# The next batch's context attention, stepped through the present batch's tail in a fused decoder layer

## The reference

```python
def layer(x, ctx):                                   # per batch
    # 1. self attention, 16 heads of 16, with clipped relative positions (+-20)
    h = layernorm(x)
    attn = softmax((q @ k.T + q . rel_k[idx]) / 4)
    x = x + (attn @ v + attn . rel_v[idx]) @ Wo.T + bo
    # 2. context attention WITHOUT softmax: 16 heads of 64
    Qn = layernorm(layernorm(x)) * g1 + b1
    Kn = layernorm(ctx) * g1 + b1                    # 1601 rows
    qn, kn = l2norm(Qn @ wq), l2norm(Kn @ wk)        # by head
    out = (qn @ kn.T) @ (Kn @ wv)                    # = qn @ (kn.T @ Kn @ wv)
    y = Q + out @ wo + bo
    x = x + y + gelu(layernorm(y) * g2 + b2 @ w1 + b1) @ w2 + b2
    # 3. gated FFN, inputs and weights rounded blockwise (16) to FP4 values
    z = quant(layernorm(x))
    x = x + quant(silu(z @ wg.T) * (z @ wu.T)) @ wd.T
```

## Time and profile before

| | us |
|---|---|
| median of 3 runs | 3678.69 |
| lowest, highest | 3668.11, 3689.46 |
| profiled execution | 3670.19 |
| its span, first to last instruction | 3668.3 |
| period of the loop over the batches | 440.3 |

### The profile page before, as it was taken

The page is one execution under the profiler, slowest core; times in us unless marked ns, Lnnn a source line. Parts: engine busy times, 40 slices in busy tenths (PEclk is TensorE's granted clock), DMA queues, the critical chain, the costliest instruction groups (busy, mean ns, idle before and its releaser), DMA issues.

```text
span 3668.3 us, 48646 instructions
## 1 busy us (share of the span) xinstructions
PE 2691.3 (73%) x14836; PEld 1813.0 (49%) x14884; DVE 1985.8 (54%) x4001; ACT 1195.6 (33%) x1925; POOL 1153.9 (31%) x812
## 2 busy tenths in 40 slices
PE   0487777877787776867768777687777867787776
PEld 0255544554455544555445545355544554455544
DVE  5646465463754537545375554646455464654537
ACT  1226222271233612344123432225223271233611
POOL 1352223422243123521235222362223522244122
PEclk9999988998899987998879989799888998899987
DMA  6365004650056400663008520364104650056400
GB/s 195 34 127 135 20 6 53 123 145 7 2 85 124 112 6 13 100 128 82 6 18 127 120 58 6 32 137 126 28 6 48 128 141 6 8 76 127 118 6 6
DMA packets 503886, 259.07 MB, mean 71 GB/s; under 512 B 213166, under 2 KB 501702, under 8 KB 502598
## 3 DMA queue, kind: packets, MB, share of 16 engines
q1 hardware_dynamic: 436982, 221.53, 31.0%
q10 hardware_dynamic: 66560, 33.56, 4.0%
HBM read 129.67 MB, written 125.35 MB: 70 GB/s over the span
## 4 chain that ended last, share of the span: by engine, by line
PE 50%; DVE 19%; issue 10%; ACT 8%; POOL 4%; DMA 4%; ACTq 1%; DVEq 1%; POOLq 0%; another core or an unknown queue 0%
PE PS L1273 44%; PE PS L1276 7%; DMA bias_scr<-M 4%; DVE arena L422 3%; ACT arena L862 2%; ACT arena L869 2%; DVE arena L427 2%; DVE arena L419 2%; POOL rn L367 1%; POOL rstd L367 1%; POOL arena L439 1%; DVE PS L1115 1%; DVE arena L424 1%; DVE arena L1072 1%; DVE arena L429 1%
## 5 line engine op out<-in xcount | busy, mean ns | idle before, releaser
L1276 PE MATMUL PS<-ident,arena 128*128 128x128 f32 (+1 forms) x3356 | 571.3, 299 | 628.5 <-POOL arena L439 289.8
L1276 PEld LDWEIGHTS PS<-ident,arena 128*128 128x128 f32 (+1 forms) x3356 | 410.9, 152 | 822.4 <-POOL arena L439 313.0
L1273 PE MATMUL PS<-arena 128*17 128x128 f32 (+5 forms) x6624 | 729.5, 318 | 106.6 <-ACT arena L869 60.1
L1273 PEld LDWEIGHTS PS<-arena 128*17 128x17 f32 (+2 forms) x6656 | 510.2, 126 | 214.1 <-ACT arena L869 68.1
L367 POOL TENSOR_TENSOR rn<-rn,mhalf 128x16 f32<-128x16 f32 (+1 forms) x136 | 412.9, 3036 | 475.0 <-DVE rn L1065 264.7
L1115 DVE CUSTOM_DVE_ANT_0 PS<-PS,arena 128x512 f32<-128x512 f32 x512 | 343.2, 712 | 97.0 <-PE PS L1273 68.9
L1273 PE MATMUL PS<-cwk,arena 128*128 128x512 f32 (+1 forms) x832 | 376.1, 595 | 23.7 <-ACT arena L801 21.0
L862 ACT ACTIVATE arena<-PS,nmax 128x512 f32<-128x512 f32 x512 | 352.1, 690 | 74.3 <-DVE nmax L1115 65.5
L716 POOL TENSOR_TENSOR arena<-arena,mass_mask 128x512 f32<-128x512 f32 x128 | 163.3, 1276 | 571.9 <-ACT arena L862 571.9
L367 POOL TENSOR_TENSOR rstd<-rstd,mhalf 128x1 f32<-128x1 f32 (+3 forms) x153 | 104.0, 680 | 719.6 <-DVE rstd L380 300.9
L1063 DVE TENSOR_REDUCE ss<-arena 128x16 f32<-128x1024 f32 (+1 forms) x104 | 126.9, 1220 | 285.1 <-ACT arena L807 285.1
(11 more groups left out here) (163 smaller groups left out, 3763.2 us busy)
## 6 DMA issues: line engine op xcount, KB each, us to landing
arena<-bias_scr SPq DMA_DIRECT2D x128, 336.0 KB, 3.2
prob_scr<-arena SPq DMA_DIRECT2D x128, 336.0 KB, 3.7
bias_scr<-M ACTq DMA_DIRECT2D x64, 512.0 KB, 4.8
q_scr<-arena SPq DMA_DIRECT2D x128, 128.0 KB
arena<-k_scr SPq DMA_DIRECT2D x64, 256.0 KB, 10.9
arena<-q_scr SPq DMA_DIRECT2D x128, 128.0 KB, 3.2
arena<-in_ctx SPq DMA_DIRECT2D x96, 128.0 KB, 2.5
arena<-far_scr SPq DMA_DIRECT2D x64, 182.0 KB, 17.0
```

The costliest lines, as they stand in the source:

```text
L1273: return pe.matmul(o, l, r, start=start, stop=stop, **kw)
L1276: return pe.transpose(o, i, ident[0:i.shape[0], 0:i.shape[0]])
```

## The change

The context of a batch no longer stands in a stage of its own. While batch b is in its tail, the engines work on the context of batch b+1, and while b is in its FFN, they run the finale and the preparation of b+1. Batch 0 gets its context and preparation ahead of the loop. The loop also does this work for a ninth batch of zeros (`ctx` and `x` are padded), in the last turn.

- The context runs in two passes of half the heads each: 26 steps (`CSTEPS`) with 512 projected columns and 4 matmuls into two banks of `G` (4, 5). Norm and transposition of a row tile are done in the first pass only; all 13 normed tiles stay in SBUF. The second pass waits until the banks have been copied out (`evac_g`).
- One pipeline turn over all engines is a `slot(nb, s)`, s from -6 to 25. `SLOTS_AT` says behind which piece of the tail each engine runs which slots. A slot on PE is the projection of step s+3, the transposition of tile s+4 and the `G` matmuls of step s; on DVE it is statistics of tile s+6, head sums of step s+2, norm of tile s+5, scaling of step s+1.
- The tail uses PSUM banks 0 to 3 (and half of 7) in place of eight: `project_q` has one pair of banks, not two.
- The finale is laid between the four tiles of the second MLP matmul. Then come `norm_x(b+1)`, the projections, the splits (`first_rests`, `second_rests`, `middle_parts`, `last_parts`), strewn between the rounding steps of x. `gate_up` comes behind them.
- SP's list for b+1 is `prepare`: band stores, all part stores, a wait for `parts_stored`, then the loads of `Kp`, `Qp`, `Kfar`, and only then the stores of the far edges, which ACT issued before. There are 16 of them now, of 128 x 512 (`Eb` has half the room).
- POOL makes the 16 far edges in the rounding loop, four behind each tile's `quant_divide` and `quant_finish`.

```diff
+SLOTS_AT = {("band", 0): (-6, -5), ("band", 1): (-4,), ("band", 2): (-3,), ("band", 3): (-2,),
+            ("wo", 0): (-1,), ("wo", 1): (0,), ("wo", 2): (1,), ("wo", 3): (2,), "ln": (3, 4, 5, 6),
...
+            "yn": (19, 20, 21), ("h", 1): (22,), ("h", 3): (23,), ("h", 5): (24,), ("h", 7): (25,)}
...
 # POOL
                 for t in range(T + 1):
                     if t < T:
                         pool.wait_ge(quant_s, 2 * (T * b + t + 1) + 1)
                         pool.sem_inc(waits_alone, 1)
-                        quant_divide(pool, gs[:, t, :], t % 2, 128, FF)
+                        quant_divide(pool, gs[:, t % 2, :], t % 2, 128, FF)
                     if t:
...
+                        quant_finish(pool, st, qc[:, (t - 1) % 2, :], (t - 1) % 2, 128, FF, NQ0 + b * QPB + NXQ + t - 1)
+                    if t < T:
+                        for g in range(NG):
+                            far_edge(b + 1, t, g)
...
+            def far_edge(nb, t, g):
+                if t == 0 and g == 0:
+                    pool.wait_ge(r_act, 2 * T * (nb + 1) + 1)
...
+                    pool.wait_ge(part2_ready, 2 * (nb + 1) + 1)
...
+                pool.wait_ge(eb_stored[g % 2], 16 * (2 * (T * nb + t) + g // 2) + 1)
...
+                pool.tensor_tensor(Eb[:, g % 2, :, :], tail_mask[:].unsqueeze(1).broadcast_to([128, HG, 128]),
+                                   bcast(Rb[:, t, g * HG:(g + 1) * HG, BAND], 128), ALU.mult).then_inc(eb_ready, 1)
 # PE, FFN
+                second(0)
+                transpose_g(b + 1)
+                second(1)
+                key_values(b + 1)
+                second(2)
+                context_out(b + 1)
+                second(3)
+                project_x(b + 1)
...
 # DVE, FFN
+                add_x2(3)
+                norm_x2(0)
+                norm_x(b + 1)
+                quant_count(dve, st, 0, 128, XQ * E, NQ0 + b * QPB)
+                norm_x2(1)
+                first_rests(b + 1)
+                quant_count(dve, st, 1, 128, XQ * E, NQ0 + b * QPB + 1)
+                second_rests(b + 1)
                 for t in range(T + 3):
...
+                    if t == 0:
+                        last_parts(b + 1)
```

More of the change, by code:

```diff
@@ L851, in exps, with slots @@
+            all_slots(slot, 0)
+            evac_g(0, 1)
+            copy_gt(0)
+            copy_m(0)
+            project_x(0)
+            for t in range(T):
+                copy_r(0, t)
+            middle_parts(0)
+            with act.Fori(0, NB) as b:
+                def slots(at):
+                    for s in SLOTS_AT[at]:
+                        slot(b + 1, s)
                 def exps(t, h):
@@ L1102, in _, with slots @@
-                dve.wait_ge(m_act, 4 * (b + 1) + 1)
-                dve.sem_inc(waits_alone, 1)
+            all_slots(slot, 0)
+            evac_g(0, 1)
+            copy_gt(0)
+            mask_kv(0)
+            copy_m(0)
+            norm_x(0)
+            first_rests(0)
+            second_rests(0)
+            last_parts(0)
+            with dve.Fori(0, NB) as b:
+                def slots(at):
+                    for s in SLOTS_AT[at]:
+                        slot(b + 1, s)
                 def bias(t, h):
@@ L1241, in _, with norm_x2 @@
+                def norm_x2(i):
                     some = range(XQ * i, XQ * (i + 1))
[L1242 to L1245 removed]
                     dve.wait_ge(x2_ready, T * b + XQ * (i + 1) + 1)
```

1004 lines of the change are left out of this document (517 added, 487 removed), and 1 row of the table SLOTS_AT.

## The result

The changed kernel takes **4235.7 us** (median of 4 runs, 4233.5 to 4238.4) against 3676.1 for the kernel before (4 runs beside it): a ratio of 1.152, 95% interval 1.148 to 1.155. Forecast were 4080 us and a range of 3850 to 4240. The sign and the mechanism were right; the loss was 560 us in place of 410. The time lies only 4 us inside the upper end of the range, and outside the 3950 to 4160 that the prediction gave the forecast itself.

The account below looks back on a forecast made before the run. PE bounds the context stage, engine-to-engine chains bound tail and FFN. Startup 358 + 8 x (attention 5.5 + 96.5, tail 181.5, FFN 180) + 12 = 4078, predicted 4080 us, 11% slower; range 3850 to 4240.

Parts of the forecast that it names:

- The mechanism: FFN rounding loop: POOL stands at the third far edge until the first edge's store lands behind SP's part stores and loads.
- FFN up to the rounding: FFN start: finale and preparation stand ahead of gate_up; first quant_divide at τ = 75.5 where it was 36, last_parts ends at 79.
- The chain of DMAs: SP's queue in the FFN: stores from τ = 79 to 94, loads at 166 GB/s to 121, edge store landed at 124.
- The pitches: FFN rounding loop: edges add 2 us to the old pitch of 12.1; tiles take 13, 14.5 and 11.5, FFN ends at 180.
- rival 4: FFN rounding loop: edges lock DVE for their full 0.96 us each, FFN 11 us longer, 4168 us; chance 14%.
- The tail: Tail with context slots: 66 + 79 + 14 + 22.5 = 181.5 us, 83 more than before; PE clock near 1.0, busy for 155.
- Attention's start: Attention: same work, 96.5 us, plus 5.5 because first windows load only after the last out has landed.
- Startup and end: Ahead of and behind the loop: first attention near 358 us, stores and loads 42, edges 35; 12 us for the end.
- rival 1: Tail and rounding loop: PE reaches its floor of 160 us in the tail, the rounding loop stalls; 3908 us, chance 10%.
- rival 2: FFN: the chain of DMAs doesn't hold POOL, FFN 137 us, tail as forecast; 3736 us, chance 6%.
- rival 3: Tail and FFN: tail of 160 us and FFN of 137 together, period 399, faster at 3552 us; chance 6%.
- rival 5: Tail: slots wait for each other, context runs as if in its own stage; tail 207 us, 4280 us, chance 6%.

Follow-up runs that it names:

- kernel 1: Changed kernel with the 16 far edges placed behind the last quant_finish on POOL, SP's list unchanged: 4048.4 us, 1.102 of the kernel before.
- kernel 2: Changed kernel with the far edges' stores issued on ACT's queue, buffers and POOL's order unchanged: 3962.5 us, 1.079 of the kernel before.
- kernel 5: Changed kernel with four far-edge buffers in place of two, SP's list and POOL's order unchanged: 4137.3 us, 1.125 of the kernel before.
- kernel 12: kernel 10 with each far edge made by four ACT activations in place of one POOL product: 3658.6 us, 0.996 of the kernel before.
- kernel 9: Changed kernel with edge stores on ACT's queue, four buffers, early windows, no ninth batch, zero matmuls around the bands, ACT's copies ahead of edge stores: 3666.9 us.
- kernel 7: Changed kernel with zero matmuls on PE where it waits at the end of attention and in the bands: 4178.9 us, 1.137 of the kernel before.
- kernel 3: Changed kernel without context slots and finale in the loop, the M of batch 0 serving all turns: 3547.2 us, 0.964 of the kernel before.
- kernel 6: Changed kernel with both the edges' stores on ACT's queue and four edge buffers: 3848.7 us, 1.047 of the kernel before.
- kernel 10: kernel 9 with zero matmuls in PE's waits in the FFN as well: 3657.5 us, 0.995 of the kernel before.
- kernel 11: The kernel before, without the change, with zero matmuls in PE's waits of tail and FFN: 3684.4 us, 1.004 of the kernel before.

## Why the prediction was right, and where it was too low

**The mechanism.** Right in each link: third edge held, with it the second division, the first finish and `down`; released by a store behind 22 stores and 20 loads. Idle time forecast 40 to 50 us, measured 53.4. Kernels 1, 2 and 5 take away the place of the edges, the place of the stores, and the wait, and each gives what its link is worth.

**FFN up to the rounding.** First `quant_divide` at τ = 75.2 (75.5 forecast), last splits 79, as forecast.

**The chain of DMAs, the term that was mis-sized.** Forecast: stores 15 us, loads 27, the edge's landing 3, τ = 124. Measured 17.5, 24 of issue, and 14 to the landing, τ = 134.5. The rates in the stretches of part stores and of loads (second and third line):

```profile
1225.00:1240.00 15.00, 1.84 (x7) 0.81 (x5) 9.45 (x15) 0.76 (x1) 2.01 (x2) 0.72 0.63 206
...
1243.00:1260.00 17.00, 0.00 (x0) 0.00 (x0) 0.00 (x0) 0.00 (x0) 0.00 (x0) 0.50 1.11 114
1260.00:1277.00 17.00, 0.00 (x0) 0.00 (x0) 0.00 (x0) 0.00 (x0) 0.00 (x0) 0.50 1.24 129
```

The loads moved 114 to 129 GB/s with the DMA engines full, not the 166 of the earlier trace rows: 4.1 MB took 34 us. The 166 was the rate of two queues together. Here are the queues in the stretch of the earlier trace rows, and in that of the loads now (1243 to 1277 us); q1 is SP's, q10 ACT's:

```profile
q1 hardware_dynamic: 6014, 4.05, 88.8%
q10 hardware_dynamic: 3039, 1.54, 26.9%
...
q1 hardware_dynamic: 6490, 4.13, 117.4%
```

The loads' own 4.05 MB took the whole 33.7 us in the kernel before too, 120 GB/s, with 1.54 MB of edge stores beside them. The forecast had them go faster without these stores, and they did not. That is 8 us for the loads and 2.5 for the stores, and they went through to the end: FFN 190.7 in the turn shown and 189.7 in the mean, in place of 180, 8 x 9.7 = 78 of the missing 158 us. The Trainium skill, DMA: Bandwidth & Descriptors, Bandwidth, has small transfers far below the peak; that holds here. The 341 GB/s by which the prediction had weighed 3920 us is the page's figure for a larger transfer, and these of 128 to 256 KB stayed far below it.

**The pitches.** 14.2, 14.4 and 12.3 us between the finishes (13, 14.5, 11.5 forecast), 36.2 in all in kernel 1 and 40.9 here. So the edges cost DVE's chain 4.7 us for three tiles. That is 1.9 more than the 39 us forecast, where rival 4 had 11 more: it was too dear, though DVE does lose time in steps. First its pair L437 in kernel 12, whose edges are ACT's: beside one of POOL's products, and undisturbed; then in kernel 9 L409 and the pair.

```profile
1149.71 2.89 DVE L437 SCALAR_TENSOR_TENSOR arena<-arena 128x704 f32<-128x704 f32 x2
...
1186.78 1.82 DVE L437 SCALAR_TENSOR_TENSOR arena<-arena 128x704 f32<-128x704 f32 x2
```

```profile
1142.02 0.19 DVE L409 TENSOR_SCALAR qhs<-qsc 128x44 f32<-128x44 f32 x1
...
1162.33 0.91 DVE L409 TENSOR_SCALAR qhs<-qsc 128x44 f32<-128x44 f32 x1
...
1165.92 3.95 DVE L437 SCALAR_TENSOR_TENSOR arena<-arena 128x704 f32<-128x704 f32 x2
```

L409 takes 0.91 us in place of 0.19 while POOL works on four edges (1161.11 to 1165.49). They also push POOL's division back, so that the pair meets two of POOL's products and takes 3.95. By the Trainium skill, SBUF — State Buffer, Who interferes with whom, the one that holds the shared ports keeps the other out for a whole instruction; the steps of 1.07 us from 1.82 to 2.89 and 3.95 agree with that.

**The tail.** Forecast 181.5, mean 188, of which the first part 75.2 for 66, the rest 112.8 for 115.5. The failed step is "With full queues PE stays at the faster level": the first part was summed from DVE's work, and in each of the eight turns PE ran two or all four of its bands at 1.2 GHz. Kernel 7, in which PE is kept at 2.4 GHz, has 66.4. The whole tail, 188.3 between bands, is 8 x 6.8 = 54 us of the missing 158. The sign for the tail failed as well: PE was busy for 177 of 190.5 us (167 of 179 in kernel 7), not for 155 of 180, so the tail is nearer to being PE's own than the forecast had it. That kernel 7 meets the 66 us for the first part may be luck: DVE is busy there for 46.5 us, and the sum counted 56 of it. The four banks, which cost 12 us without slots (kernel 3), have no term in the sum; what they cost with slots beside them no run shows.

**Attention's start.** Attention and its start were put at 102 us and took 105.3 in the mean: 8 x 3.3 = 26 us. In the turn shown the bias waits 10.69 us for its window, 5.5 were added for it. In the changed kernel SP issues the window 3.9 us after the landing of `out`; in kernel 2 it is 0.9. No row shows what lies between; this stays open.

**Startup and end.** First attention at 380.7 for 358. The same chain, stores and loads, was put at 42 us and took 67, behind four band stores of 320 KB which the sum forgot (10 us of issue). The edges took 28 for 35. The end: 12 us were added, and the last turn, behind which no windows are waited for, is shorter than the others; span less startup less eight turns is 4236.6 - 380.7 - 8 x 483.2 = -9.7, so the sum was 22 us too high there. Together 22.7 + 8 x 19.7 - 21.7 = 158.6, the whole difference to 4078.

**The rivals.** Rival 1 needed a tail of 160 us, rival 2 a chain that doesn't hold POOL, rival 3 both; none came. Kernel 6, which removes the stall, has 3848.7, above the 3736 of rival 2. Its FFN takes 148 us where that rival has 137: from its first finish to the fourth it is 45.3 us, and PE waits 4.8, 5.5 and 8.0 us for ACT's copies, which stand behind the edges' stores in ACT's list. Its tail takes 187. Rival 5 (a tail of 207) was nearer than rival 1: 188. The time itself lies between rival 4 (4168) and rival 5 (4280), but by neither mechanism: it is the forecast's mechanism with the chain of DMAs, the clock in the bands and the startup put too low.

## What to carry to other kernels

When a step moves behind another one, follow every queue it passes: an operation that waits for a free buffer belongs to the length of the queue in which that buffer's store stands, and the engine on which it waits takes along all that is listed behind it. Stores that free a buffer go on another queue than long lists of loads. More buffers alone move such a wait on by the tiles that they cover (12.2 us of a turn here, 13.2 on top of the other queue) and don't remove it. A DMA rate is carried over only from transfers of the same kind and counted by queue, and a stretch that becomes PE's own is counted at either clock.

## What the runs showed of the hardware

- Loads from DRAM in transfers of 128 to 256 KB with packets below 2 KB moved 114 to 129 GB/s at a DMA share of 1.1 to 1.2; the part stores 206 GB/s at 0.63.
- A store on another queue than the part stores and loads doesn't wait for their list: the store of the first edge landed 5.5 us after the edge was made from ACT's queue beside the part stores, and 55 us after it from SP's queue, where it was issued 41 us after the edge was made and then took 14 among the loads in flight. The Trainium skill, DMA: Bandwidth & Descriptors, Issuing engines are not separate DMA queues, says that a second issuing engine saves only the time of the issue, usually small; here that time, and the loads queued ahead, were worth 33 us a turn (kernel 2). Among the loads POOL's wait was 17.5 us with the stores on ACT's queue too.
- In the bands PE's clock fell to 1.2 GHz behind a stretch of 47.7 us at 2.4 GHz in which it was busy for 34.5 and never idle for more than 2.3 us at a time, and stayed there while it was busy for 5.00 of 5 us; 32 matmuls of zeros (12 ahead of the bands, 20 among them) kept it at 2.4. Where PE waits for others, fillers raised the clock and gave no time in the turn (kernels 10 and 11).
- The issue of two stores held ACT for 3.8 us in kernel 12, and with it the copies listed behind.
